# The expert loop of an attention-and-MoE layer takes two token tiles for each load of the weights

## The reference

```python
x = x + attn(layernorm(x))
x = x + ffn(layernorm(x))
# attn, 16 heads of 64: decayed linear attention without softmax
scores = (Q @ K.T) * Dm / 8;  out = scores @ V
c = groupnorm(out)          # per head, mean and variance over ALL 4096 tokens
return c @ Wout
# ffn: 8 experts, the best 2 of a softmax over 8 logits, and a shared expert
out = sum_e combine[:, e] * ((silu(x @ w_gate[e]) * (x @ w_up[e])) @ w_down[e])
out += sigmoid(x @ sg) * ((silu(x @ sw_gate) * (x @ sw_up)) @ sw_down)
```

## Time and profile before

| what | us |
|---|---|
| the two executions shown | 6445.14, 6522.21 |
| their median | 6483.67 |
| the profiled execution | 5907.06 |
| its span, slowest core | 5905.5 |
| spans of the 8 cores | 5879.4 to 5905.5 |
| PE busy in the span | 4999.4 |
| start of phase 2's first transposes | 1183.26 |
| first Wout matmul of the second and third tile | 1783.24, 2371.14 |

### The profile page before, as it was taken

One profiled execution on the slowest core, in us unless ns is written; L12 is line 12 of the kernel. 1 busy time (PEld: TensorE's weight loads), 2 busy tenths in 40 slices (PEclk: granted clock), 3 DMA queues, 4 the chain that ended last, 5 costly groups with the idle time before them and its releaser, 6 DMA issues.

```text
span 5905.5 us, 65504 instructions; the slowest of 8 cores (5879.4 to 5905.5 us)
## 1 busy us (share of the span) xinstructions
PE 4999.4 (85%) x24644; PEld 2333.5 (40%) x24644; DVE 1437.7 (24%) x3601; ACT 1439.4 (24%) x3555; POOL 190.7 (3%) x333
## 2 busy tenths in 40 slices
PE   3555555489998999899989998999899989998999
PEld 1333333234443444344434443444344434443444
DVE  1454544421112112211221122112211221122111
ACT  1343444231213121312131213121312131213121
POOL 0000000000000000000000000000000000000000
PEclk9666666689999999999999999999899999998999
DMA  8777777624333434343434343434342433342433
GB/s 169 179 179 175 180 183 178 185 83 157 137 145 126 157 137 151 120 169 125 157 122 169 118 157 123 168 118 157 124 167 118 159 132 157 120 159 110 155 119 130
DMA packets 101251, 867.26 MB, mean 147 GB/s; under 512 B 9552, under 2 KB 9552, under 8 KB 65360
## 3 DMA queue, kind: packets, MB, share of 16 engines
q0 software_dynamic: 76048, 787.00, 40.0%
q1 hardware_dynamic: 24896, 76.09, 4.0%
HBM read 837.91 MB, written 103.02 MB: 159 GB/s over the span
## 4 chain that ended last, share of the span: by engine, by line
PE 70%; DMA 5%; ACT 3%; DVE 1%; issue 1%; ACTq 0%; POOL 0%; DVEq 0%; SPq 0%; POOLq 0%
PE psf L1002 23%; PE psf L1006 23%; PE psf L1063 21%; DMA wring<-wbf 4%; PE psf L865 2%; ACT silu_sb L1018 1%; ACT xln_bf L161 1%; DMA x_sb<-x 1%; ACT ucp_sb L1019 1%; DVE h_sb L1028 0%; PE psb L778 0%; DVE xln2T L792 0%; PE psb L752 0%; DVE combT L761 0%; ACT L151 0%
## 5 line engine op out<-in xcount | busy, mean ns | idle before, releaser
L1063 PE MATMUL psf<-wring,h_sb 128*128 128x512 bf16 x6336 | 1452.5, 393 | 138.2 <-DVE h_sb L1028 138.2
L1002 PE MATMUL psf<-xln2T,wring 128*128 128x512 bf16 x6336 | 1510.0, 381 | 10.3 <-DMA wring<-wbf 9.9
L1006 PE MATMUL psf<-xln2T,wring 128*128 128x512 bf16 x6336 | 1499.9, 380 | 0.0
L1018 ACT ACTIVATE silu_sb<-psf 128x512 bf16<-128x512 f32 x792 | 473.0, 597 | 3294.6 <-PE psf L1006 3294.5
L1063 PEld LDWEIGHTS psf<-wring,h_sb 128*128 128x128 bf16 x6336 | 633.2, 101 | 954.8 <-issue 266.7
L1028 DVE TENSOR_TENSOR h_sb<-silu_sb,ucp_sb 128x512 bf16<-128x512 bf16 x792 | 336.9, 425 | 2438.0 <-ACT ucp_sb L1019 2438.0
L1002 PEld LDWEIGHTS psf<-xln2T,wring 128*128 128x128 bf16 x6336 | 620.8, 98 | 767.6 <-issue 31.2
L1006 PEld LDWEIGHTS psf<-xln2T,wring 128*128 128x128 bf16 x6336 | 621.3, 98 | 752.2 <-issue 8.3
L1079 DVE SCALAR_TENSOR_TENSOR x_sb<-psf,c_sb,x_sb 128x512 f32<-128x512 f32 x576 | 432.7, 751 | 1099.7 <-PE psf L1063 1099.7
L1019 ACT CAST ucp_sb<-psf 128x512 bf16<-128x512 f32 x792 | 459.5, 580 | 0.0
L254 PE MATMUL psb<-eye_sb,xln_bf 128*128 128x128 bf16 x256 | 32.4, 302 | 320.2 <-ACT xln_bf L161 313.9
(11 more groups left out here) (102 smaller groups left out, 1871.5 us busy)
## 6 DMA issues: line engine op xcount, KB each, us to landing
wring<-wbf POOLq DMA_DIRECT2D x216, 2816.0 KB, 12.3
wbf<-stg POOLq DMA_DIRECT2D x36, 1408.0 KB, 5.6
x_sb<-x SPq DMA_DIRECT2D x64, 512.0 KB, 6.7
stg<-wg POOLq DMA_DIRECT2D x16, 1408.0 KB, 11.2
stg<-wu POOLq DMA_DIRECT2D x16, 1408.0 KB, 11.3
out<-x_sb SPq DMA_DIRECT2D x32, 512.0 KB, 14.8
wbf<-stg POOLq DMA_DIRECT2D x9, 1536.0 KB, 6.2
stg<-wd POOLq DMA_DIRECT2D x8, 1536.0 KB, 12.6
```

What stands on the lines that cost most here:

```text
L1002: t.matmul(gb, wring[:, wg0 + dt * IFF + it * C:wg0 + dt * IFF + (it + 1) * C], xln2T[:, dt * SC:(dt + 1) * SC], start=(dt == 0), stop=(dt ...
L1006: ins = t.matmul(ub, wring[:, wu0 + dt * IFF + it * C:wu0 + dt * IFF + (it + 1) * C], xln2T[:, dt * SC:(dt + 1) * SC], start=(dt == 0), st ...
L1018: sc.activation(silu_sb[:, (it % 2) * SC:(it % 2 + 1) * SC], gb, AF.Silu)
L1063: ins = t.matmul(db, h_sb[:, hb + it * SC + tloc * C:hb + it * SC + (tloc + 1) * C], wring[:, wd0 + it * D + dc * 512:wd0 + it * D + (dc + ...
```

## The change

NPIECES becomes 27 x 4. The loop goes over 4 pairs of tiles. The prephase, now the function `emit_prephase(t_i, xln2T_dst, first_pair)`, is written for both tiles of the pair, one after the other; its `emit_combT_all` and the place in the last expert are gone, and both tiles make `combT` at the start of their prephase. The first tile's normalised, transposed input goes to `xln2T`, the second's to `combT`, which is free once that tile's Wout matmuls are done. `c8_sb` has a half for each tile. In the expert loop each expert does a unit for the first tile and then one for the second with the same pieces; the next pieces are fetched only after the second (`if tp == 1`). The loads of x are issued for both tiles at once, at the head of a pair's code, and the stores of a pair stand at its end. Some small buffers of phase 1 move to that phase's pool, which makes room.

```diff
-NPIECES = PPT * NTILE
+NPIECES = PPT * (NTILE // 2)
...
-        c8_sb = sb2("c8_sb", [C, 4 * NEXP], F32)
+        c8_sb = sb2("c8_sb", [C, 2 * 4 * NEXP], F32)
...
-                if e == NEXP - 1 and t_i + 1 < NTILE:
-                    petn, vctn = emit_combT_all(pipe2["ldc_tgt"])
...
+            emit_t512b(combt_sb, combT, s12[:, 0:8], s12[:, 8:16])
...
-            emit_t512b(xln2_bf, xln2T)
+            emit_t512b(xln2_bf, xln2T_dst)
...
-            emit_trt(0)
+            emit_trt(0, wait_scr=router_sc_tgts.get(t_i - 1))
...
+        for pair in range(NTILE // 2):
+            t0, t1 = 2 * pair, 2 * pair + 1
...
+                def ldx2(s, t0=t0, wtgt=wout_done_hist[t1 - 2], tgt=S("sld").n):
+                    s.wait_ge(S("vcw").h, wtgt)
+                    for tp in range(2):
+                        for tt in range(4):
+                            ins = s.dma_start(
+                                out=x_sb[:, tp * 4 * D + tt * D:tp * 4 * D + (tt + 1) * D],
+                                in_=x_h[(t0 + tp) * SC + tt * C:(t0 + tp) * SC + (tt + 1) * C, :])
+                            ins.then_inc(S("sld").h, 16)
+                    s.wait_ge(S("sld").h, tgt)
+                em("sync", ldx2)
+                xpair_tgt = S("sld").n
+                em("vector", lambda v, tgt=xpair_tgt: v.wait_ge(S("sld").h, tgt))
+
+            emit_prephase(t0, xln2T, pair)
+            emit_prephase(t1, combT, pair)
...
+                p0 = PPT * pair + 3 * e
+                for tp in range(2):
+                    t_i = t0 + tp
+                    u = unit_idx[0]
+                    hb = (u % 2) * NIT * SC
+                    xT = xln2T if tp == 0 else combT
...
+                    if tp == 1:
+                        piece_done[p0] = ("scg", S("scg").n)
+                        piece_done[p0 + 1] = ("scg", S("scg").n)
...
+            for tp in range(2):
+                t_i = t0 + tp
+                x1 = x1_sb[:, (t_i % 2) * 4 * D:(t_i % 2 + 1) * 4 * D]
+                tile_done = S("vcd").n - (8 if tp == 0 else 0)
```

More of the change, by code:

```diff
@@ L95, in build_nc @@
     eye = sb("eye_sb", [C, C], BF16)
-    gnwb = sb("gnwb_sb", [C, 16], F32)
     wout_bf = sb("wout_bf", [C, 8 * D], BF16)
@@ L175, in build_nc @@
         gcols = sb1("gcols_sb", [C, 2 * NH], F32)
+        gnwb = sb1("gnwb_sb", [C, 16], F32)
+        statm = sb1("statm", [C, 32], F32)
+        srow = sb1("srow", [1, 32], F32)
+        srow2 = sb1("srow2", [1, 16], F32)
+        onecol = sb1("onecol", [C, 1], F32)
+        onerow = sb1("onerow", [1, C], F32)
         wq_bf = sb1("wq_bf", [C, 8 * D], BF16)
@@ L739, in build_nc @@
         next_piece = 3
[L741 to L767, removed]
         def emit_t512b(src_t, dst, scale_cols=None, shift_cols=None):
@@ L795, in emit_t512b, with emit_prephase @@
                 em("vector", tev)
-        store_tgts = []
+        store_tgts = {}
         wout_done_hist = {}
-        pipe2 = {}
-        for t_i in range(NTILE):
+        ln2_tgts = {}
+        router_tgts = {}
+        router_sc_tgts = {}
+        c8off = {}
+        def emit_prephase(t_i, xln2T_dst, first_pair):
             x1 = x1_sb[:, (t_i % 2) * 4 * D:(t_i % 2 + 1) * 4 * D]
             xcur = x_sb[:, (t_i % 2) * 4 * D:(t_i % 2 + 1) * 4 * D]
[L805 to L817, removed]
+            combx_tgt = comb_tgts[t_i]
             def twx2(t, tgt=combx_tgt, g=gn_done, first=(t_i == 0)):
@@ L826, in build_nc @@
             em("scalar", lambda sc, tgt=combx_tgt: (sc.wait_ge(S("sld").h, tgt), sc.drain()))
[L828 to L834, removed]
+            emit_t512b(combt_sb, combT, s12[:, 0:8], s12[:, 8:16])
+            combT_done = S("vct").n
+            pet_tr_done = S("pet").n
             if t_i + 1 < NTILE:
@@ L846, in build_nc @@
                 em("sync", ldc)
-                pipe2["ldc_tgt"] = S("sld").n
+                comb_tgts[t_i + 1] = S("sld").n
             vcw_tloc = []
@@ L856, in twout @@
                               ctgt=combT_done, banktgt=S("vcw").n - 1,
-                              dtgt=S("vcd").n):
+                              dtgt=(S("vcd").n if gidx == 0 else 0),
+                              rtgt=(router_sc_tgts.get(t_i - 1, 0) if gidx == 0 else 0)):
                         if gidx == 0:
@@ L861, in twout @@
                                 t.wait_ge(S("vcd").h, dtgt)
+                            if rtgt >= 1:
+                                t.wait_ge(S("scr").h, rtgt)
                         if banktgt >= 1:
@@ L873, in vwout @@
                     def vwout(v, tloc=tloc, dc=dc, bk=bk, tgt=S("pew").n, x1=x1, xcur=xcur,
-                              sttgt=(store_tgts[t_i - 2] if (gidx == 0 and t_i >= 2) else None)):
+                              sttgt=(store_tgts.get(t_i - 2) if gidx == 0 else None)):
                         v.wait_ge(S("pew").h, tgt)
@@ L887, in build_nc @@
             wout_done_hist[t_i] = wout_done
[L888 to L903, removed]
-            emit_t512b(xln2_bf, xln2T)
+            ln2_tgts[t_i] = emit_ln_sc(x1, xln2_bf, per_tt_wait=vcw_tloc)
+            em("tensor", lambda t, tgt=ln2_tgts[t_i]: t.wait_ge(S("sc1").h, tgt))
+            emit_t512b(xln2_bf, xln2T_dst)
             xln2T_done = S("vct").n
+            c0 = c8off[t_i]
             rreg = [(0, 0), (1, 0), (0, 16), (1, 16)]
```

261 lines of the change are left out of this document (137 added, 124 removed).

## The result

The changed kernel is slower: its time stands to that of the kernel before as 1.0217 (95% interval 1.0181 to 1.0254), so that it is slower is clear, and whether by more than 2% is not. In the executions that the ratio rests on, the changed kernel took 6048 to 6062 us; of the kernel before, three took 5909 to 5919 and a fourth 5956, and with that one in, the means stand as the ratio says (6052 beside 5923, +129 us). Between the lowest of each there are 139 us. The forecast was +138 us, or a ratio of 1.021. The medians over all executions are 6155.29 (13) beside 6310.31 (10): by them the changed kernel would be the faster one.

The account below looks back on a forecast made before the run. The prediction took TensorE to set the end, with weight waits of only 9.9 us. Its terms, -5 + 32 + 105 + 6 = +138 us, gave 6045 us for the profiled execution and 6622 us on the median, range 6045 to 6710.

Parts of the forecast that it names:

- Wout after the last down part: Turn between pairs: Wout starts at 1818.9 instead of 1783.24, +35.7 us, as PE waits for x and combT.
- the two prephases of a pair: Router of the first tile, then combT, Wout and router of the second: 51.6 us in place of 38.4 + 3.2, +10.0.
- expert units: Expert loop: -5 us of weight waits, -2 us a pair of cold starts, 3.2 us of hoisted transposes leaving each of 7 turns.
- start of phase 2: First load has 2.10 MB of x more beside 11.88 MB: +6 us on the path, 0 as the other bound.
- The x load: Turns between pairs: x loads stand behind the stores, PE stands still, +34.9 us at each of three, +105 us.
- The second prephase: Within a pair: it follows the first on every engine, VectorE's router ending 7.4 us late; +32 us over four pairs.
- The clock: Down parts: 1.7 us at 1.2 GHz in some 48 units may come more or less often; -80 to +40 us, taken as 0.
- Rival (c): Down parts: the 1.2 GHz stretches go away with the waits for weights; +58, 6542 us, +0.9%; chance 12%.
- part 1: Expert loop: half of the weight loads go, 108 instead of 216 pieces, saving half of 9.9 us of waits, -5 us.
- rival (a): Expert unit starts: weights were the bound in the longer executions; half the waits go, 6339 us, -2.2%; chance 10%.
- Rival (d): Whole kernel: the longer executions do not come back, so it is timed at its profile's level, 6045 us; chance 5%.
- Rival (b): Turns between pairs: x loads come sooner, 20 instead of 35 us at each of three; +95, 6579 us, +1.5%; chance 15%.

Follow-up runs that it names:

- refetch: The changed kernel with each unit fetching its three weight pieces again (216 pieces, pairs kept): ratio to the kernel before 1.025, 6054 and 6057 us.
- half_loads_old_order: The kernel before with odd tiles fetching no weight pieces (108 loads, wrong weights in the output): ratio to the kernel before 0.9995 (0.9966 to 1.0024).
- x_early: The changed kernel with the next pair's eight x loads issued ahead of the stores, behind the second prephase: ratio to the kernel before 1.008, 5950 to 5959 us.
- old_order_x_late: The kernel before, one tile at a time, with the next tile's x load moved behind this tile's store on SyncE's queue: ratio 1.0309, 6085 to 6096 us.
- interleaved: x_early with a pair's two prephases woven together, the second tile's transposes and router inside the pair's first unit: 5883.35 us in one execution, no interval.
- the router in the groups: interleaved plus next pair's first combT transposes in the last unit, and routers and second tile's transposes between the first unit's gate/up groups: ratio to before 0.9936.

## Why the prediction was right in the change and wrong in the time

The forecast in its own terms, with both profiles' core 0 (starts and ends from the timelines):

| term | predicted | measured |
|---|---|---|
| Wout after the last down part, each of 3 turns | +35.7 | +36.1 (37.2 beside 1.1) |
| the two prephases of a pair, first Wout to first expert (before: with the 1.1 us between the tiles) | +15.6 (10.0, and 3.2 and 2.4 booked at the turn); 13.2 in the first pair | +15.6 (92.6 beside 77.0); +12.3 in the first pair (90.8 beside 78.4) |
| expert units (cold starts, hoisted transposes, waits for weights) | -35 | -41 |
| start of phase 2 | +6 | +1 on core 0, +10 as a mean of cores 0 to 3 |
| sum | +138 | +127 on core 0, ratio 1.0217 |

*What bounds the kernel: right.* TensorE sets the end in both kernels. The halved traffic was worth -5 in the forecast; refetch and half_loads_old_order can't tell its worth from none. One reading was too narrow: the two loads do not fill the whole down part. The 280 GB/s of the window is a mean over its idle edges too; within it (core 0 of before, the same columns) DMA moves 341 and 352 GB/s and is 0.94 to 0.96 busy, so the comparison of 280 to 301 GB/s with a rate of streaming sets a diluted number beside it:

```profile
1394.00:1411.00 17.00, 17.00 (x77) 7.52 (x75) 4.54 (x7) 0.00 (x0) 0.00 (x0) 0.95 0.96 341
...
1699.00:1715.00 16.00, 16.00 (x76) 7.28 (x75) 4.72 (x7) 0.00 (x0) 0.00 (x0) 1.00 0.94 352
```

*The x load: right, and shown.* 31 us a turn by x_early, and the same stall without pairs by old_order_x_late (predicted 6097, measured 6085 to 6096). The size came out too: x was through 31.6 us after the last down part (2400.87) where the forecast had 31.2. The issue of eight loads was left out of it; SyncE took 9.23 us for them, the sixth and seventh alone some 5 us. Whether that lengthened the turn no run shows: the DMA engines were 89% busy meanwhile.

*The second prephase: right.* VectorE was late by 7.5 us, Wout cold at 16.62.

*The expert units: right, a little small.* Core 0's pauses in front of the down parts fell from 178.4 to 152.9 us in all (forecast -22), the waits for weights by 8.7 us (forecast -5), and the 7 us left are near the 8 of the cold starts.

*The clock: right to leave it.* The stretches at 1.2 GHz in the down part did not go: on core 0 the down parts above 20.3 us are 47 of 72, beside 43 before (the forecast had read 48 there). Rival (c) falls.

*What failed* is the step "on the median, 6622 us", in the paragraph before part 1: "I make the sum against 5907.06 and add the same difference to the median". The term was not in the profile: nothing showed what the 576.6 us were, and a sum made against 5907.06 belongs to 5907.06. There it gave 6045 us, and the changed kernel took 6048 to 6062. What stood in the term's place is how many executions had cores at a lower clock: six of the ten of before took over 6100 us, and seven of the thirteen of the changed kernel. The median of two executions was no level of this kernel; over ten it is 6310. The changed kernel's median over 13 is 6155.29, 467 us under the forecast and 155 us under the median before, against the direction of the forecast, while every term of the change cost what the sum said. That a median falls here is luck of the draw and no gain of the kernel. Why some executions have the lower clock stays open. In the changed kernel rival (a), weights as the bound of the long executions, falls with the 0.4 us of core 5; for the kernel before it is out only in so far as its core lists look alike. Rival (d), the level of the profile, was nearest in the number and had 5%; its condition, that longer executions do not come back, did not hold. Rival (b) falls with the three waits of 30.7 us.

The terms of the woven versions were oversized. Of 25 us a pair for interleaved, 17 came by its one execution. The part up to the first expert matmul came as expected; 2.6 us of the rest are the first unit's pause (15.6 instead of 13), and what the others are is open.

## What to carry to other kernels

Ask of a transfer that is to be halved what is waited for it, not how many bytes it moves: 10 us of waits was about all there was to win. When a loop is regrouped, write down each DMA queue's order before and after: here two functions that only changed places (x behind the store, later the comb load ahead of the store) cost some 90 us and some 25 to 50 us (0.9936 to 0.9877 with the router in the groups, 1.0029 to 0.9941 without). And a sum made against a profiled execution gives a ratio; it is a time only at the level of that execution, and a median over a handful of executions may say which of them were slowed and not what the change did.

## What was not expected of the hardware

- 311 MB less of weights on each core (787.00 MB on that queue before, 475.56 after) was worth nothing that refetch or half_loads_old_order could tell from none, and the long down parts did not get fewer (47 of 72 beside 43).
- Eight x loads of 512 KB took SyncE 9.23 us to issue behind four stores, where four took 1.76 us with nothing before them but loads that had landed.
